# One attention and Fourier block on one core: the first step's transfers alone, statistics in two parts, and projections placed inside rows of scores

## The reference

```python
xn = _layernorm(x, axis=-1)
x = x + _L0_attn_ref(xn, wq, wk, wv, wo) + _L0_ffn_ref(xn, w_freq_real, w_freq_imag, bias)
```

## Time and profile before

| | us |
|---|---|
| median of 3 executions | 992.09 |
| lowest, highest | 991.64, 1003.47 |
| the profiled execution | 994.67 |
| its span, from the first to the last instruction | 993.0 |
| mean granted clock of TensorE | 0.969 |

### The profile page before, as it was taken

One profiled execution on the slowest core, in us unless ns is written; L12 is line 12 of the kernel. 1 busy time (PEld: TensorE's weight loads), 2 busy tenths in 40 slices (PEclk: granted clock), 3 DMA queues, 4 the chain that ended last, 5 costly groups with the idle time before them and its releaser, 6 DMA issues.

```text
span 993.0 us, 17699 instructions
## 1 busy us (share of the span) xinstructions
PE 946.6 (95%) x6764; PEld 463.8 (47%) x6764; DVE 731.2 (74%) x894; ACT 653.1 (66%) x1302; POOL 312.9 (32%) x343
## 2 busy tenths in 40 slices
PE   8969999999999989999999999999999999999998
PEld 6744555445444334534454555444444443544424
DVE  6887677678777897787888666677778887788801
ACT  6423666646667746676777666676677765677795
POOL 4368863865238000136300223236111000100000
PEclk9858999999999989999999999999999997999999
DMA  7535132154101300010100321001410000000000
GB/s 249 134 75 92 34 85 77 34 102 112 50 7 54 60 17 1 13 49 22 49 19 3 69 58 33 22 1 34 104 37 1 2 2 1 13 11 2 1 1 22
DMA packets 37700, 43.48 MB, mean 44 GB/s; under 512 B 11376, under 2 KB 23280, under 8 KB 37616
## 3 DMA queue, kind: packets, MB, share of 16 engines
q1 hardware_dynamic: 37544, 42.35, 17.5%
q10 hardware_dynamic: 72, 0.01, 0.0%
HBM read 27.13 MB, written 14.68 MB: 42 GB/s over the span
## 4 chain that ended last, share of the span: by engine, by line
PE 46%; ACT 4%; issue 1%; DVE 1%; POOL 0%; ACTq 0%; POOLq 0%
PE psO L1387 17%; PE psS L1370 10%; PE psA L1323 10%; ACT prob_sb L986 3%; PE psS L1355 2%; PE psS L1357 1%; PE psA L1328 1%; PE psA L1370 1%; PE psA L1338 1%; PE psS L1296 1%; ACT oraw_sb L995 1%; PE psS L1347 0%; DVE pmax L1132 0%; PE psS L1303 0%; PE psA L1402 0%
## 5 line engine op out<-in xcount | busy, mean ns | idle before, releaser
L986 ACT ACTIVATE prob_sb<-psS 128x512 f32<-128x512 f32 (+2 forms) x1108 | 561.3, 589 | 210.6 <-PE psS L1370 207.7
L1134 DVE TENSOR_REDUCE pmax<-psA 128x2 f32<-128x1024 f32 x384 | 459.9, 1220 | 111.5 <-PE psA L1323 110.4
L1370 PE MATMUL psS<-q_st,k_st 50*128 50x512 f32 (+3 forms) x1232 | 392.1, 425 | 4.6 <-ACT prob_sb L986 3.8
L1323 PE MATMUL psA<-k_st,q_st 48*128 48x512 f32 (+3 forms) x1280 | 360.4, 426 | 16.5 <-DVE pmax L1132 5.6
L1387 PE MATMUL psO<-prob_sb,v_sb 128*17 128x512 f32 (+3 forms) x2560 | 301.7, 543 | 16.2 <-ACT prob_sb L986 7.8
L1323 PEld LDWEIGHTS psA<-k_st,q_st 48*128 48x128 f32 x1280 | 177.5, 193 | 242.0 <-DVE pmax L1134 87.6
L1132 DVE TENSOR_REDUCE pmax<-psA 128x4 f32<-128x512 f32 (+2 forms) x192 | 198.9, 1048 | 88.2 <-PE psA L1328 86.9
L871 POOL TENSOR_SCALAR_AFFINE_SELECT prob_sb<-prob_sb 128x512 f32<-128x512 f32 x128 | 81.1, 636 | 498.6 <-ACT prob_sb L986 484.0
L1370 PEld LDWEIGHTS psS<-q_st,k_st 50*128 50x128 f32 x1232 | 191.2, 188 | 94.1 <-ACT prob_sb L986 83.9
L1387 PEld LDWEIGHTS psO<-prob_sb,v_sb 128*17 128x17 f32 x2560 | 42.9, 95 | 105.1 <-issue 40.2
L1328 PE MATMUL psA<-mask_r,mask_l 64*128 64x64 bf16 (+1 forms) x768 | 81.9, 214 | 0.0
(11 more groups left out here) (110 smaller groups left out, 546.2 us busy)
## 6 DMA issues: line engine op xcount, KB each, us to landing
q_st<-parts_scratch SPq DMA_DIRECT2D x174, 64.0 KB, 2.2
parts_scratch<-parts SPq DMA_DIRECT2D x64, 128.0 KB
k_st<-parts_scratch SPq DMA_DIRECT2D x48, 128.0 KB, 4.3
q_st<-spartT SPq DMA_DIRECT2D x252, 2.0 KB
x_sb<-in_L_attn_x SPq DMA_DIRECT2D x7, 512.0 KB, 4.0
out<-x_sb SPq DMA_DIRECT2D x14, 256.0 KB, 2.2
parts_scratch<-parts SPq DMA_DIRECT2D x32, 64.0 KB
oraw_sb<-in_L_attn_x SPq DMA_DIRECT2D x1, 1536.0 KB, 8.9
```

The costliest lines, as they stand in the source:

```text
L986: nc.scalar.activation(prob[:, g % DEEP, r0:r0 + hp, s0:CH], bank_at(bank)[:, 0:hp * w].rearrange("p (h s) -> p h s", h=hp), ACT.Exp).then ...
L1134: nc.vector.reduce_max(pmax[:, heads[0]:heads[0] + 3:2, i, q], psA[:, two:two + 2, :], AX.X).then_inc(S["a_free"], 1)
L1323: last = mm(bank[:, k * w:(k + 1) * w], q_st[lo:lo + ROWS, n % (2 * KV), heads[o * per + k] % 2, i * P:(i + 1) * P], k_st[lo:lo + ROWS, sl ...
L1370: last = mm(bank[:, h * w:(h + 1) * w], k_st[lo:lo + FULL, key_slot(n, tile), kv, tile % CT * P:(tile % CT + 1) * P], q_st[lo:lo + FULL, n ...
```

## The change

In the opening, SyncE issues `x_two` and `x_last` after the first steps' transfers and no longer before them. Keys of chunk 0 are loaded in two parts: step 0's (6 DMAs of 32 KB) and, after `store(3)`, those of steps 1 to 3 (6 of 96 KB). ScalarE issues half of `store(2)` and half `t` = 1 of the first queries. `a_use` waits for keys in two counts. The projection of values of chunk 0 leaves the opening and is now the planner's first stage job.

Statistics of tiles 8 to 15 are done whole in the opening (`sample`, `moments`, `newton`, with ScalarE's root there). Tiles 16 to 31 are sampled after the last use of step 1 (`STATS_AT` = 1), their root comes at the first scores of step 3. ScalarE calls the exponential once on one column in the opening, into `aside_sb`. `ones_rows` of slot 1 moves behind that.

In the planner, asides may be put in when the last job was a score (`"a"` or `"b"`) and ScalarE's backlog is over 0.8 us, where it was after `values` with a backlog over 0.5. Asides as a last resort are kept out until step 0's uses are issued. Starting values for queues and readiness change.

```diff
-        pool_free, sp_free, dma_free = -6.0, 1.0, 1.0
+        pool_free, sp_free, dma_free = -5.0, 11.0, 12.0
-        q_ready, xnT_at, x_at = {n: 7.0 if n else 0.0 for n in range(KV)}, {0: 0.0, 1: 0.0}, {c: 18.0 for c in range(NJ)}
+        q_ready, xnT_at, x_at = {n: 8.0 if n else 0.0 for n in range(KV)}, {0: 0.0, 1: 0.0}, {c: 0.0 for c in range(NJ)}
-        stage = [("v", 1)]
+        stage = [("v", 0), ("v", 1)]
...
-            elif aside and pe and pe[-1][0] == "pv" and now - aside_at > 2.5 and act - now > 0.5:
+            elif aside and pe and pe[-1][0] in ("a", "b") and now - aside_at > 2.5 and act - now > 0.8:
                 choice = aside
...
-                if ready[choice] > first + 1.0 and (beside < BESIDE[step] or ready[choice] == big):
+                if next_a >= LAST_FIRST and ready[choice] > first + 1.0 and (beside < BESIDE[step] or ready[choice] == big):
...
-    ROOTS_JOB = next(job for job in PE_ORDER if job[0] == "b")
+    ROOTS_JOB = ("b", BEGIN[STATS_AT + 2], 0)
...
+            store(0)
+            store(1)
+            load_first_k(slice(0, 1))
+            store_half(2, 0)
+            first_q(sp, 0, False)
+            store(3)
+            load_first_k(slice(1, KV))
+            first_q(sp, 0, True)
+            first_q(sp, 1, True)
             sp.dma_start(x_two, x_v[:, BTILES:BTILES + TWO, :]).then_inc(S["x_two_in"], 16)
             sp.dma_start(x_last, x_v[:, BTILES + TWO:2 * BTILES, :]).then_inc(S["x_two_in"], 16)
-            store(0)
-            store(1)
-            load_k(0)
-            store(2)
-            load_first_q(0, False)
-            load_first_q(1, False)
-            store(3)
-            for rest in (True,):
-                for t in range(2):
-                    load_first_q(t, rest)
...
                 copy_qk(3 + m)
-                ones_rows(1, m)
+                if m == 0:
+
+                    act.wait_ge(S["first_parts"], 2 * FIRST.index(2) + 2)
+                    store_rows(act, 2, 1)
+                else:
+                    first_q(act, 1, False)
...
+            roots(2 * CT, 4 * CT, 2)
             copy_qk(5)
-            copy_v(0)
+            nc.scalar.activation(aside_sb[:, :], ident[:, 0:1], ACT.Exp)
+            ones_rows(1, 0)
+            ones_rows(1, 1)
...
-            sample(2 * CT, CHUNKS * CT)
+            sample(2 * CT, 4 * CT)
+            moments(2 * CT, 4 * CT)
+            newton(2 * CT, 4 * CT, 2)
             for v in range(len(SEQ_A)):
-                if v == LAST_USE[0] + 3:
-                    moments(2 * CT, CHUNKS * CT)
+                if v == LAST_USE[STATS_AT] + 1:
+                    sample(4 * CT, CHUNKS * CT)
+                    moments(4 * CT, CHUNKS * CT)
                 if v == ROOTS_BACK:
-                    newton(2 * CT, CHUNKS * CT, 2)
+                    newton(4 * CT, CHUNKS * CT, 3)
...
             project_qk(5)
             pe.wait_ge(S["wv_in"], 16)
-            project_v(0)
```

62 lines of the change are left out of this document (43 added, 19 removed).

## The result

The kernel after took 1003.97 us in the median of 20 runs (997.70 to 1009.27), the kernel before 997.95 (20 runs, 991.04 to 1025.29). The ratio is 1.0066, with a 95% interval of 1.0039 to 1.0092: 0.7% slower, less than the 2% that decides between same and slower. The forecast was 985, 0.7% faster than the 992.09 that it started from. The ratio leaves out executions more than 1.5% above the fastest of their kernel, which takes away the long tail of the kernel before (up to 1025 us) and nothing of the kernel after. Over all executions whose clocks are known, the mean span is 1001.2 us for 134 of the kernel before and 1001.4 for 32 of the kernel after.

The account below looks back on a forecast made before the run. TensorE (busy 95%) was taken to bound the kernel, losing time where it waits or runs at 1.2 GHz. From 992.1 us, -5 for the opening and -2 for the middle gave 985; forecast 980 to 990, range with rivals 973 to 998.

Parts of the forecast that it names:

- Keys in two parts: Opening: splitting the keys takes 3.8 us of bytes from the queue; first use starts at 40.5, 3.6 us earlier.
- Values in the pause: Between steps 0 and 1: chunk 0's value projection, 1.9 us of work, is covered by the pause and costs nothing.
- Opening statistics: VectorE in the opening: 8 tiles, `moments`, root and `newton` take 4.6 us from 36, ending 40.6, just hidden.
- Step 1: Opening: step 1 starts at 53.5 us, 2.7 earlier; its shift is ready at 61.1, 5.8 earlier.
- The x transfers: Opening, behind the queries: 5.4 us, landing at 59; step 0's shift lands at 62.6, first scores at 62.7, 4.2 earlier.
- rival that the transfers eat the gain: Opening: step 0's shift lands after 67 or step 1's queries at 56 as before; 990 to 994 us, chance 0.17.
- Second statistics: VectorE after step 1: 6.4 us of samples and `moments`, no cost, since step 2's shift waits on SyncE's queue.
- Carry to 102: From the opening to 102 us: 4.5 to 5 us of the 5.8 us lead are carried on.
- Roots at step 3: ScalarE at step 3: one more table change there and back, 2.8 us, taken as 0 because of slack.
- The order of the middle: Middle: moving some 36 asides from behind `values` to behind scores gives -2 us, between +6 and -8.
- rival that asides in rows make it slower: Middle: asides used up early leave TensorE at VectorE's pace and 1.2 GHz; two more low stretches give 1002, chance 0.13.
- Clock 0.97 to 0.98: Whole span: as few low-clock stretches as before, with a mean granted clock of 0.97 to 0.98.

Follow-up runs that it names:

- o_pv: a_old_stats with the planner's old rule for asides (behind values, backlog over 0.5): ratio 1.0011 to the kernel before, 969.8 us at equal clock.
- b_ab: Kernel before with only the planner's new rule for asides (behind scores, backlog over 0.8): ratio 0.9999, 962.2 us at equal clock.
- a_pv: Kernel after with the planner's old rule for asides put back: ratio 1.0150 to the kernel before, 976.2 us at equal clock.
- a_old_stats: Kernel after with old statistics and x transfers, without the early exponential and the planner's allowances: ratio 0.9963 to the kernel before, 963.6 us at equal clock.
- a_x_first: Kernel after with x_two and x_last issued ahead of the stores, planner told so, statistics still split: ratio 1.0107, 969.5 us at equal clock.
- b_stats: Kernel before with only the split statistics, the planner's 6.5 us for them and the early exponential: ratio 1.0106, 977.0 us at equal clock.
- o_values: a_old_stats with the values of chunk 0 back in the opening and a separate semaphore for the second keys: ratio 1.0005, 964.8 us at equal clock.
- a_plan: Kernel after without the planner's 6.5 us allowance for the samples after step 1: ratio 1.0104 to the kernel before, 973.6 us at equal clock.
- a_exp_root: Kernel after with Exp in place of step 3's square root, saving two table loads: ratio 1.0045 to the kernel before, 968.9 us at equal clock.
- a_x18: Kernel after with only the planner's readiness times for x put back from 0 to 18: ratio 1.0071, 967.1 us at equal clock.
- o_fill: a_old_stats with 16 unread matmuls ahead of the first use and a separate semaphore for the second keys: ratio 0.9938, 966.2 us at equal clock.

## Why the prediction was wrong, point by point

The sum was -5 for the opening, -2 for the order, 0 for the statistics. At equal clock the runs give 0 (o_pv), -7 (b_ab, a_pv) and +6 to +8 (a_old_stats, a_x_first, b_stats), together 0: after 969.2, before 969.1. Two steps failed. The split of the statistics was put at nothing, and it costs 6 to 8 us. And the opening's lead of 5 us, carried on to 102 and from there to the end, is worth nothing at the end even without the split (o_pv 969.8). The third, the order, was sized too small, and its larger gain hid the loss: that the result is near the kernel before is luck. Of the 19 us between forecast and median, 7 are these terms and 6 the starting point (last paragraph of this section); the other 6 are between two medians of 20, and the means over all executions (1001.2 and 1001.4) don't show them.

*What bounds the kernel.* TensorE stays at 96%, as expected.

*Keys in two parts.* 3.8 us of bytes were taken as 3.8 us of time. In the other profiles with split keys the first use came at 41.69 to 43.86, 0.3 to 2.4 us earlier than in the earlier trace rows; in the profiled execution of after it was not earlier at all. Queries bound it, as the step had it, but `store(3)` and the second keys now run beside the last of them. The Trainium skill's DMA: Bandwidth & Descriptors, section Issuing engines are not separate DMA queues, holds that issuing from a second engine saves only time to issue; the trace agrees: ScalarE's three loads were issued from 38.80 to 40.1, 2.2 us ahead of SyncE's in the kernel before, and landed at 44.1, no earlier than those at 43.9.

*Values in the pause.* Costed at 0, though the pair takes 7.09 us at 1.2 GHz; in the kernel after they end at 56.8, where step 1 starts. In o_values the pause was bound by queries (54.15), 1.3 us earlier than in a_old_stats, and worth nothing at the end. So the 0 held at the end, though not for the reason given: the pause did not cover them.

*Opening statistics.* Expected end 40.6; it was 43.7. They began at 36.6 and not at 36, and root and `newton` took 3.7 us (from 40.0) and not 1.3. Hidden, as the last queries of the first use landed at 44.1.

*Step 1.* Start 56.69 for 53.5, shift 64.9 for 61.1. Both are 3.2 to 3.8 late: the first use came 3.9 later than expected, and the pair of projections then filled the pause to its end.

*The x transfers.* Landing by 59 was right within 2.6 us (issued at 45.54 and 46.01, landed 13.7 and 15.6 us later), but `store(4)` behind them took 6.83 us instead of 3.4. The half that decided was not on SyncE: ScalarE's issue stood behind two copies at 67.0. First scores 71.2 for 62.7, which is the condition of the rival that the transfers eat the gain, and the prediction's own sign of being wrong. The rival's place was right, its mechanism wrong, and its price too: a_x_first had first scores at 63.5 and gained nothing.

*Second statistics.* The 6.4 us of VectorE after step 1 were put at 0, because "Step 2's maxima are not needed sooner". What the runs show in its place is a cost of 6 to 8 us, by itself on the kernel before too (b_stats). That it comes through step 2's maxima is not shown: a_plan had that shift at 75.9, 11 us earlier than the profile of the kernel after, and was slower. The step looked at SyncE's queue for one shift and not at what follows: the planner, told of 6.5 us, wrote another order for all later steps. What the duration does and what the order does is open: shortening the samples within the old order, or dropping the allowance with long samples, gave nothing or a loss.

*Carry to 102.* In the kernel after the earlier starts of steps 0 and 1 were gone by 82: TensorE was busy 5.5 us more from 42 to 67 and 4 less from 67 to 82. In o_pv, without the split, a lead of 3.8 us reached the shift of step 4 at 104.6, so there the carry held, and the error is in taking it as a gain of the whole: 0.9 us of it was left at step 5, and nothing at the end.

The sign that the clock would be back at 2.4 GHz by 78 failed as well (0.50 from 67 to 82).

*Roots at step 3.* 0 was right (a_exp_root 968.9).

*The order of the middle.* -2, with bounds +6 and -8; it measured -7 at equal clock, near the lower bound. The Trainium skill, TensorEngine Tiling (Array Packing), section Tiling Modes, Key Properties, says that a change of tiling mode drains TensorE. The turn towards the upper bound that the prediction drew from it did not come: with more asides inside rows the kernel is faster at equal clock; what one change costs, no run here shows. The rival that asides in rows make it slower fell with b_ab and a_pv.

*Clock 0.97 to 0.98.* It was 0.947 in the profile, 0.957 by the mean of the 20. The kernel before has the same mean, 86 us at 1.2 GHz; of the three runs that the forecast started from two were short ones of it, and so was the profiled one (62 us at 1.2 GHz). That alone is 6 us of the miss: as a ratio, the forecast was 0.993 and the result 1.0066.

## What to carry to other kernels

Work that "fits beside" another engine is not free because the next queue waits anyway: 6.4 us moved out of the opening into VectorE's list cost 6 to 8 us, and neither its length nor its place ahead of step 2's maxima explained them alone. A lead in an opening is not yet a gain: 3.8 us at 105 us were 0.9 at 132 and nothing at the end, so look for it at several later marks. When a trace names a wait, check when the thing named had really landed; a shared semaphore gave the name of keys to a wait for queries. And test each part alone on the kernel before: here +7 and -7 hid each other.

## What the chip showed that was not expected

Executions of one program spread over 9 us (a_x18) to 38 us (the kernel before), nearly all of it going with the granted clock: o_fill from 985.5 at 0.972 to 1007.6 at 0.946. The clock was at 1.2 GHz in stretches where TensorE was busy throughout (16.98 of 17 us from 127 to 144 in the kernel after), and filling a wait ahead of a low stretch put the fall off by some 3 us and no more. A us at 1.2 GHz went with 0.37 us of span, and not the 0.5 of an engine that is always the bound. A difference of 5 us between orders could be read only after taking that out.
